# One transformer block on one core: the router's logits by expert in the later halves, batch 1's projections moved among the maxima, the last output projection half a pass later

## The reference, cut to what matters

```
def expert_choice_ffn(x, gate_w, w_gate, w_up, w_down):     # B=4, S=1024, D=128, 8 experts, I=512
    affinity = softmax(x @ gate_w.T)                        # over the 8 experts
    gating, idx = top_k(affinity.transpose(0, 2, 1), 256)   # each expert takes 256 tokens of each batch
    x_in = x[idx]
    h = silu(x_in @ w_gate.T) * (x_in @ w_up.T)
    return zeros.at[idx].add(gating * (h @ w_down.T))

x = x + 0.5 * expert_choice_ffn(layernorm(x))
x = x + attention(layernorm(x))   # 16 heads of 8, 3D rotary turn of q and k, softmax over 1024 keys, then Wo
x = x + 0.5 * expert_choice_ffn(layernorm(x))
```

## Time and profile before

| | |
|---|---|
| median of 3 executions | 1208.99 us (1207.38 to 1209.43) |
| the profiled execution | 1207.35 us, of it 1205.3 us span |
| start, first halves' front | 0 to 66 us |
| first expert layer | 66 to 298.5 us |
| window, 44 pieces of the maxima | 298.5 to 362 us |
| attention's main loop | 362 to 962 us |
| second expert layer, last scatter ends | 971 to 1198.5 us |
| busy: TensorE, VectorE, ScalarE, GpSimd | 1088.2, 918.8, 769.6, 600.1 us |

### The profile page before, as it was taken

One profiled execution on the slowest core, in us unless ns is written; L12 is line 12 of the kernel. 1 busy time (PEld: TensorE's weight loads), 2 busy tenths in 40 slices (PEclk: granted clock), 3 DMA queues, 4 the chain that ended last, 5 costly groups with the idle time before them and its releaser, 6 DMA issues.

```text
span 1205.3 us, 23761 instructions
## 1 busy us (share of the span) xinstructions
PE 1088.2 (90%) x8900; PEld 478.3 (40%) x8900; DVE 918.8 (76%) x1510; ACT 769.6 (64%) x1461; POOL 600.1 (50%) x619
## 2 busy tenths in 40 slices
PE   6199999898599999999999999999998889999993
PEld 6167666565132222222222222222222256666762
DVE  5745855465979999999999999999997554854441
ACT  3054322432368999999989999899999836222220
POOL 4046888775378511100003447455430187677886
PEclk6579999999598999999999999999999988999997
DMA  9025456458514220212111222112310125345553
GB/s 274 32 60 115 91 112 136 88 118 198 135 37 123 61 64 19 58 46 58 40 29 40 52 52 62 25 40 58 81 45 8 31 79 130 83 92 101 114 101 30
DMA packets 93065, 93.95 MB, mean 78 GB/s; under 512 B 14684, under 2 KB 70108, under 8 KB 92920
## 3 DMA queue, kind: packets, MB, share of 16 engines
q1 hardware_dynamic: 70424, 75.66, 22.6%
q0 software_dynamic: 22528, 16.79, 10.3%
HBM read 64.22 MB, written 30.13 MB: 78 GB/s over the span
## 4 chain that ended last, share of the span: by engine, by line
DVE 43%; PE 35%; issue 11%; POOL 5%; ACT 4%; DMA 1%; SPq 0%; DVEq 0%; POOLq 0%; another core or an unknown queue 0%; ACTq 0%
DVE mx L1877 38%; PE pA L1329 7%; PE pS L1317 7%; POOL out_dram L655 3%; ACT Pt L1154 3%; PE pO L1318 3%; PE pS L1318 3%; PE pO L1469 3%; DVE ge L1564 2%; PE pS L1490 2%; PE pA L1297 2%; PE pS L1235 2%; POOL xg L632 1%; PE pA L1405 1%; PE pA L1235 1%
## 5 line engine op out<-in xcount | busy, mean ns | idle before, releaser
L1877 DVE TENSOR_REDUCE mx<-pA 128x2 f32<-128x1024 f32 x512 | 585.2, 1217 | 13.8 <-PE pA L1405 13.0
L1154 ACT ACTIVATE Pt<-pS 128x512 f32<-128x512 f32 x1024 | 556.3, 596 | 30.9 <-PE pS L1490 25.0
L1469 PE MATMUL pO<-Pt,Vst 128*16 128x256 f32 x4096 | 321.5, 386 | 12.5 <-ACT U L1145 12.5
L1049 ACT ACTIVATE Pt<-pS 128x512 f32<-128x512 f32 x128 | 76.4, 597 | 199.9 <-PE pS L1317 176.6
L632 POOL DMA_INDIRECT xg<-zd,idx x128 | 128.4, 1003 | 149.4 <-DVE idx L1684 76.3
L1405 PE MATMUL pA<-Kst,Qst 48*128 48x512 bf16 x704 | 140.9, 397 | 20.1 <-DVE mx L1877 18.9
L1469 PEld LDWEIGHTS pO<-Pt,Vst 128*16 128x16 f32 x4096 | 68.0, 94 | 204.3 <-issue 107.2
L1317 PE MATMUL pS<-Pt,wg 128*128 128x512 f32 x256 | 139.7, 628 | 4.5 <-DVE Pt L1711 2.1
L1490 PE MATMUL pS<-Qst,Kst 51*128 51x512 bf16 x704 | 138.6, 390 | 5.1 <-issue 1.0
L722 POOL TENSOR_TENSOR mparts<-mx,onesm 128x32 bf16<-128x32 f32 x16 | 4.0, 252 | 267.1 <-DVE mx L1882 210.9
L1329 PEld LDWEIGHTS pA<-wd,Pt 128*128 128x128 f32 x960 | 113.5, 192 | 16.8 <-issue 16.8
(11 more groups left out here) (229 smaller groups left out, 1214.7 us busy)
## 6 DMA issues: line engine op xcount, KB each, us to landing
wg<-w_gate_dram SPq DMA_DIRECT2D x32, 256.0 KB
wu<-w_up_dram SPq DMA_DIRECT2D x32, 256.0 KB
wd<-w_down_dram SPq DMA_DIRECT2D x32, 256.0 KB
qk<-parts SPq DMA_DIRECT2D x64, 96.0 KB
Kst<-qk SPq DMA_DIRECT2D x132, 32.0 KB
zd<-Z SPq DMA_DIRECT2D x8, 512.0 KB
vp<-pair SPq DMA_DIRECT2D x4, 1024.0 KB, 4.6
Vst<-vp SPq DMA_DIRECT2D x16, 256.0 KB
```

Source lines behind the costliest of these rows:

```text
L1049: S.activation(sg[:, u % 2, :], pG[u % 2], ACT.Silu).then_inc(s_silu, 1)
L1154: S.activation(Pt[:, s % 4, j, r * 512:(r + 1) * 512], pS[:, bank_of(k, 4 * s + 2 * j + r), :], ACT.Exp, scale=SCALE).then_inc(s_exp, 1)
L1469: last = M.matmul(pO[32 * h:32 * h + 16, cols], Vst[k][:, s % 8, h, :], Pt[:, s % 4, h // 2, (h % 2) * 512 + 256 * a:(h % 2) * 512 + 256 * ...
L1877: V.reduce_max(mx2[:, k, 2 * j:2 * j + 2, c, half], pA[ring[q, a] % 2][:, :, :], AX.X).then_inc(s_Ar, 1)
```

## The change

Five edits.

1. `veps` is gone: the root is taken of the variance itself, with 1e-5 as the activation's bias, from a tile `eps` that GpSimd fills at the start.
2. For the second half of each layer (hh = 1 and 3) the logits come with the experts on the rows: `gate_t`, padded to 32 columns, is the weight, and 512 tokens at a time are streamed, four such matmuls in four column tiles of the array. ScalarE moves the bank to SBUF, and four transposes at n = 4 turn it. The new use `("g", hh)` stands at (1, 4) and (18, 4).
3. The projections of u = 2 and 3 leave passes 14 and 15 (`("s", 15)` to `("s", 24)`) and stand in the window, behind pieces 0 to 13. VectorE's eight multiplications and two sums for them go to ScalarE (8 moves) and GpSimd (4 products, 2 sums).
4. `("p", 3, 0)` goes from (16, 2) to (16, 4), `("p", 3, 1)` from (16, 4) to (17, 1). VectorE's and ScalarE's work around them follows. Of `("f", 3, n)`, n = 2 to 5 go later, and the search takes five gaps of passes 20 and 21 in place of four.
5. On SyncE `store_values(0)` goes behind `load_weights(15)`, `store_values(1)` behind the loads of x, `load_weights(18)` ahead of `write_out(3)`.

```diff
@@ tables
+    place[1, 4] = ("g", 1)
-    for m in range(5, 25):
+    for m in range(5, 15):
         place[divmod(55 + m, 5)] = ("s", m)
-    place[16, 2], place[16, 4] = ("p", 3, 0), ("p", 3, 1)
-    for n, at in enumerate([(17, 3), (17, 4), (18, 0), (18, 1), (18, 2), (18, 4)] + [(19, k) for k in range(5)] +
-                           [(it, k) for it in (20, 21) for k in range(4)] + [(22, 0), (22, 1)]):
+    place[16, 4], place[17, 1] = ("p", 3, 0), ("p", 3, 1)
+    for n, at in enumerate([(17, 3), (17, 4), (18, 2), (18, 3), (19, 0), (19, 1)] + [(19, k) for k in range(2, 5)] +
+                           [(it, k) for it in (20, 21) for k in range(5)] + [(22, 0), (22, 1)]):
         place[at] = ("f", 3, n)
+    place[18, 4] = ("g", 3)
...
-    for u, at in ((4, 22), (5, 28), (6, 32), (7, 37)):
-        for i in range(4):
-            window[divmod(at + i, 32)] = ("PR", u, i)
+    for u, ats in ((2, (0, 2, 4, 6)), (3, (8, 10, 12, 13)), (4, range(22, 26)), (5, range(28, 32)), (6, range(32, 36)), (7, range(37, 41))):
+        for i, at in enumerate(ats):
+            window[divmod(at, 32)] = ("PR", u, i)
@@ SyncE
-            store_values(0)
             store_parts(0)
             load_weights(15)
+            store_values(0)
             store_parts(1)
             load(0)
             load(1)
-            store_values(1)
...
+            store_values(1)
             store_parts(2)
...
+            load_weights(18)
             write_out(3)
-            load_weights(18)
@@ GpSimd
             scatter(RUN - 1)
+            product(2, 0)
+            product(2, 1)
+            add_products(2)
+            product(3, 0)
             rest(2)
+            product(3, 1)
+            add_products(3)
+            lowest(2)
             rest(3)
-            lowest(2)
             lowest(3)
@@ ScalarE
-                S.activation(sd[:, tiles(i)], veps[:, tiles(i)], ACT.Sqrt).then_inc(s_sd, 1)
+                S.activation(sd[:, tiles(i)], mv[:, tiles(i), 1], ACT.Sqrt, bias=eps[:, 0:1]).then_inc(s_sd, 1)
...
+                if key and key[0] == "g":
+                    act.wait_ge(*written(key))
+                    S.activation(by_expert, sidebank, ACT.Copy).then_inc(s_room, 1)
...
+            for u in (2, 3):
+                for i in range(4):
+                    projected(u, i)
+                value_rows(u)
+            high(2)
             deviation(6)
+            middle(2)
             deviation(7)
@@ TensorE
+            def logits_by_expert(hh):
+                bank, sem = open_bank(("g", hh))
+                pe.wait_ge(*was_read(("f", hh, 3)))
+                for g in range(4):
+                    last = M.matmul(bank[32 * g:32 * g + 32, :], gate_t[:, :], ZT[:, g * 512:(g + 1) * 512], start=True, stop=True,
+                                    tile_position=(0, 32 * g))
+                last.then_inc(sem, 1)
...
-                pe.wait_ge(*was_read(("s", 24) if j < RUN else ("f", 3, NF - 1)))
+                pe.wait_ge(*was_read(("s", 14) if j < RUN else ("f", 3, NF - 1)))
...
-            pe.wait_ge(s_vs, 4)
+            pe.wait_ge(s_vs, 6)
@@ VectorE
                 for n in ts:
                     last = V.bn_aggr(mv[:, n, :], stats[:, n % CH, :])
-                link(last)
-                V.tensor_scalar(veps[:, tiles(i)], mv[:, tiles(i), 1], EPS, None, ALU.add).then_inc(s_ve, 1)
+                last.then_inc(s_ve, 1)
```

More of the change, by code:

```diff
@@ L113, in program @@
         stats = sb("stats", [P, CH, 6], F32)
-        veps = sb("veps", [P, T], F32)
+        eps = sb("eps", [P, 1], F32)
         sd = sb("sd", [P, T], F32)
@@ L217, in program @@
         num, den = scr[:, 0:2, :], scr[:, 2:4, :]
-        pairs = {4: (scr[:, 0, :], scr[:, 2, :]), 5: (scr[:, 1, :], scr[:, 3, :]), 6: (room[:, 0, :], room[:, 1, :]),
-                 7: (U[1][:, :], U[2][:, :])}
+        pairs = {u: (scr[:, u % 2, :], scr[:, 2 + u % 2, :]) for u in range(2, 6)}
+        pairs |= {6: (room[:, 0, :], room[:, 1, :]),
+                  7: (U[1][:, :], U[2][:, :])}
         dens = sb("dens", [P, P], F32)
@@ L1107, in _ @@
             normalise(6)
+            high(3)
             turned_half(0)
             turned_half(1)
+            middle(3)
             normalise(7)
@@ L1202, in front @@
                     if hh:
[L1203 to L1207, removed]
+                        pe.wait_ge(*was_read(("g", hh)))
+                        for k in range(4):
+                            last = M.transpose(bank[:, k * P:(k + 1) * P], by_expert[:, k * P:(k + 1) * P], ident[:, :])
+                    else:
+                        for k in range(CH, HT):
+                            if k % 4 == 0:
+                                pe.wait_ge(*was_read(("f", 0, k // 4)))
+                            last = M.matmul(bank[:, k * E:(k + 1) * E], ZT[:, k * P:(k + 1) * P], gate_t[:, 0:E], start=True, stop=True)
                 elif n < 7:
@@ L1277, in use @@
                     front(key[1], key[2])
+                elif key[0] == "g":
+                    logits_by_expert(key[1])
                 elif key[0] == "s":
@@ L1387, in _ @@
                     pe.wait_ge(*was_read(("f", 0, k // 4)))
-                M.matmul(bank_of_use(("f", 0, 4))[:, k * E:(k + 1) * E], ZT[:, k * P:(k + 1) * P], gate_t[:, :], start=True, stop=True)
+                M.matmul(bank_of_use(("f", 0, 4))[:, k * E:(k + 1) * E], ZT[:, k * P:(k + 1) * P], gate_t[:, 0:E], start=True, stop=True)
             for n in range(2, 8):
@@ L1429, in window_use @@
                     if i == 0:
-                        pe.wait_ge(s_winr, win["T", 2 * (b - 2) + 1] + 1)
-                    last = project(op, (wq, wr)[i // 2], 2 * (b - 2) + i % 2, bank)
+                        pe.wait_ge(*(was_read(("s", 4)) if b == 1 else (s_winr, win["T", 2 * (b - 2) + 1] + 1)))
+                    last = project(op, (wq, wr)[i // 2], 2 * (b % 2) + i % 2, bank)
                 else:
@@ L1437, in window_use @@
                     u = key[1]
[L1438 to L1439 removed]
+                    if u > 2:
+                        pe.wait_ge(s_vs, u - 2)
                     project_values(u, pO[:, :]).then_inc(s_v, 1)
@@ L1546, in moments @@
                 ts = range(i % B * CH, (i % B + 1) * CH)
+                if i:
+                    dve.wait_ge(s_ve, nth(i) - 1)
                 for n in ts:
@@ L1584, in front @@
                 if n == 4:
-                    logits = bank[:, 0:HT * E].rearrange("p (t e) -> p t e", e=E)
-                    link(V.reduce_max(lmax[:, :], logits, AX.X))
-                    V.tensor_tensor(lsub[:, :, :], logits, lmax[:, :].unsqueeze(2).to_broadcast([P, HT, E]),
-                                    ALU.subtract).then_inc(signal_read(key), 1)
+                    if hh:
+                        logits = bank.rearrange("p (j g r) -> p g j r", j=4, g=4)[:, :, :, 0:E]
+                    else:
+                        logits = bank[:, 0:HT * E].rearrange("p (g j e) -> p g j e", j=4, g=4)
+                    largest_of = lmax[:, :].rearrange("p (g j) -> p g j", j=4)
+                    link(V.reduce_max(largest_of, logits, AX.X))
+                    V.tensor_tensor(lsub[:, :, :].rearrange("p (g j) e -> p g j e", j=4), logits,
+                                    largest_of.unsqueeze(3).to_broadcast([P, 4, 4, E]), ALU.subtract).then_inc(signal_read(key), 1)
                     affinities(hh)
```

49 lines of the change are left out of this document (25 added, 24 removed).

## The result

The changed kernel takes 1198.72 us (median of 4, 1197.10 to 1199.40) against 1208.96 us: the ratio is 0.9916, with a 95% interval from 0.9898 to 0.9933. That is 10.2 us less, where 12.1 were forecast, and the time lies in the range. The profiled execution has a span of 1195.3 us, with a mean granted clock of 0.953.

What follows compares the result with a forecast made beforehand. VectorE was taken to bound the attention and TensorE the expert layers, GpSimd close behind. The terms -0.6 - 2.0 - 7.0 - 2.5 = -12.1 gave 1195.25 us for the profiled execution, 1196.9 for the median; range 1190 to 1204.

Steps and rivals of the forecast that it cites:

- The root without its addition: At the kernel's start, VectorE's addition of 0.69 us ahead of ScalarE's root goes: -0.6 us.
- later uses stand beside other work: Dropping the addition at roots after the kernel's start was taken to gain 0.
- Logits by expert: First layer: the logits' 3.49 us on TensorE become 1.10 plus 0.43 for transposes: -2.0 us, from 0 to -2.5.
- Passes 14 and 15: Batch 1's projections leave these passes, so the maxima start at 290.0 instead of 298.54: -8.5 us.
- the wait for `load(0)`: Before the maxima: the load would land some 4 us after TensorE is ready, between 288.5 and 292.5.
- TensorE's 10.1: What TensorE alone would gain from passes 14 and 15, with the maxima starting at 288.5: 10.1 us.
- SyncE's reordered stores: They have free stretches around them: 0, if the values' stores land before the maxima's values are used.
- The window: Attention's start, with the moved projections: some run at half clock, GpSimd's work fits: +1.5 us, from 0 to +4.
- the 7.0 of the sum: Net of moving batch 1's projections into the window: -7.0 us, from -10 to -2.
- Second layer: Later last projection and new logits: -0.8 + 1.9 - 5.3 + 1.7 = -2.5 us, from -6 to 0.
- the attention's start gives back: Rival, 1201 to 1205 us: late `load(0)`, GpSimd's 2.3 us margin used up, half clock costing +4; chance 0.15.
- the half clock through the whole window: Rival: TensorE stays at half clock in the whole window, +28.8 us there, 1224 in all; chance 0.07.

Runs made afterwards that it cites:

- a_veps: The changed kernel without edit 1, so VectorE adds the constant again before each root: 1197.78 us, ratio 0.9925 to the kernel before.
- b_proj: The kernel before with edit 3 alone, plus only the move of `store_values(1)` that it needs: 1202.45 us, ratio 0.9966.
- a_sum_early: The changed kernel with VectorE's last sum of batch 0's parts one gap sooner and its store ahead of the last down weights' load: 1196.95 us, ratio 0.9913.
- a_again: The changed kernel timed and profiled once more, with no edit: 1198.16 us, ratio 0.9923 to the kernel before.
- best_a: a_sum_early with the window's two shift operations reading the reciprocal from PSUM, written there by one more reciprocal each: 1192.77 us, ratio 0.9884.
- best_b: The same as best_a, with edit 4 taken back: 1191.33 us, ratio 0.9872 to the kernel before.

## Why the prediction was right, and where it was not

**The root without its addition, -0.6.** In this pair of profiles the front is 0.55 shorter. But in kernels that are alike there it is from 0.7 us longer to 1.0 shorter than before's, and a_veps is no slower. The size was right for the operation and can't be told in the time. What I priced at nothing, "later uses stand beside other work", is wrong: in the window the addition waits for GpSimd (1.78 us in b_proj, 1.98 in a_veps, for 0.17).

**Logits by expert, -2.0.** 2.4 to 2.5 us between the compactions of passes 1 and 2 in all ten kernels that have it. The group takes 1.07 us, next to the 1.10 estimated from the earlier trace rows; the rest is the idle before the old logits. So the tiling rule of the Trainium skill ("TensorEngine Tiling (Array Packing)", Key Properties) costs no more here than the 0.09 us by which the group begins later (91.49) than the next matmul would, 0.86 behind 90.54.

**Passes 14 and 15, -8.5, and the wait for `load(0)`.** The mechanism was right: TensorE's 10.1 is reached in a_sum_early, and in the changed kernel a wait of 3.85 us for the load takes part of it, leaving 7.2 to 7.7. What I mis-sized is how much sooner the load comes. The compaction of pass 13 is 5.2 us sooner than before. VectorE's sum of the parts gains 2.4 us on that (I had up to 3), and SyncE's store starts with its end:

```profile
264.39 1.13 DVE L1736 TENSOR_SCALAR Pt<-pA,gain 128x128 f32<-128x128 f32 x4 [2.34 <-PE pA L1366]
265.43 1.22 DVE L1787 TENSOR_TENSOR parts<-scr,parts 128x1024 bf16<-128x1024 f32 x1
```

But the eight issues of this store take 5.54 us (5.36 in a_again), where they took 3.89, so that `load(0)` begins at 275.13 for 280.91, only 0.5 us more than the 5.2 sooner. In a_sum_early they take 3.90 again. Why they took longer is open. The sum itself still stood behind a scaling that had waited 2.34 us for the down projection. And SyncE's reordered stores, for which I had 0, probably carry a part, as b_proj's pass 15 shows.

**The window, +1.5 from the clock.** Size near (+2.2 and +2.3; +1.1 to +3.6 over the five kernels with this window), cause in good part wrong. I counted GpSimd's time and asked only whether it would finish (34.6 us after the start; my own terms add up to 34.8). It finished later, with its first product 39.8 us after the start (36.9 before), and nothing on TensorE waited for it. I did not ask what it would do to VectorE while it runs: the shifts cost 1.8 us more, in each of the five. The trace of the kernel before had shown it, in pass 17, where GpSimd writes the second half of its `Z` from 996.76 to 997.80:

```profile
996.84 0.98 DVE L1560 SCALAR_TENSOR_TENSOR shift<-mv,rstd 128x8 f32<-128x8 f32 x1
```

The clock's part at the start is the two slow projections ahead of 291.23, by their excess over 1.13 some 1.2 us at most. What differs between the five goes with the clock from 31 to 41 us after the first piece, where TensorE is full: 0.50 in the longest window (67.4), 0.63 in this one, 0.70 in the shortest (64.9). Together with the load this makes the net of edit 3 5.0 and 5.4 us in the two profiles and 4 to 6 in the timed kernels, for the 7.0 of the sum.

**Second layer, -2.5.** This step failed: the stretch is no shorter. From the first score matmul to the last scatter the stretch took 834.6 and 831.7 us in the two kernels in which it is unchanged (before, b_proj), and 832.5 to 834.8, mean 833.7, in seven with both edits. The single terms came: the wait for GpSimd's `Z` came (4.46 us), with a clock of 0.50 behind it, the logits and the half clock behind them went, and the search's waits grew by 1.6 us (4.15 for 2.53 from pass 19's compaction on), where I had 1.7. (From the compaction of pass 19 to that of pass 22 all nine profiles with edit 4 are 2.6 to 3.1 us longer than before's, the four others without it are from 0.4 shorter to 0.1 longer; what is not waits is in part steps of the front that edit 4 moves into this stretch.) What I had not is 1.24 us for the gathered tokens and 1.4 us by which GpSimd reaches `Z` later than TensorE's shift would have it (the starts on TensorE are 10.8 us sooner at 949.94, and 9.4 at 988.14). Its tree of sums before that took longer in this profile: 3.13 and 4.71 us for the groups that took 2.28 and 3.61. The single sums that stretched ran beside VectorE's `tensor_tensor` operations with two SBUF inputs: one of 0.26 us took 0.76 beside `room<-slots,place_in`. That these are the operations which edit 4 moved is not shown: in b_proj, without edit 4, the groups took 2.99 and 4.44 us. Which of edits 2 and 4 gives what in this layer stays open to about 1.5 us: kernels alike in it differ by more.

**Why the total was right** is then partly luck: 2.5 forecast for the second layer and 2 too many for edit 3 were missing, and 0.9 us in pass 0, 2.0 in pass 11 and 0.5 more at the logits came in unforecast in this profile, less 0.7 in the first layer's search. By the timed kernels edit 2 is worth 4.7 to 5.5 us in all, where the profiles show 2.5 and an uncertain rest.

Of the rivals, that the attention's start gives back was true in part, for the load and not for GpSimd's margin; the half clock through the whole window did not come, since the clock was 1.00 from 292 to 302 already.

## What to carry to other kernels

When work is moved onto an engine that rests, ask not only whether it is done in time but what it holds while it runs: six operations that met no deadline problem stretched two tiny ones, on the engine that bounds the stretch, sixfold. An operand in PSUM took them out of its way for 0.4 us. Look in the old profile for the same operation beside the same engine: it stood there with 0.98 us. When the bound engine is relieved, follow the next one back to the instruction that releases it, and to what is queued in front of that: here a load waited for a store, the store for a sum, and the sum stood behind a scaling that waited for TensorE. And profile one kernel twice before a difference of 2 us between two profiles is explained.

## What the runs showed of the hardware

A small VectorE operation with two SBUF inputs that starts while a GpSimd `tensor_tensor` runs ends with it (310.87 beside 310.84, 313.28 beside 313.26, 310.92 beside 310.90), and doesn't wait if one of its inputs lies in PSUM (0.16 us, twice in best_a and twice in best_b). A larger one waits too: in the kernel before the 128x512 product of the context, for which TensorE waited 3.21 us, took 2.25 us beside a GpSimd operation, and 0.69 us without one. `reduce_max` from PSUM, the batch statistics and the reciprocal kept their times. The Trainium skill says this in "SBUF — State Buffer", Who interferes with whom (a VectorE instruction with two SBUF inputs contends with a GpSimd instruction that reads SBUF, and the second to issue blocks), and the trace agrees in every case; I had read it ahead of the prediction as a rule about `reduce_max`, which never contends, and left it out. The `tensor_scalar` with one SBUF input was held up too (0.37, 1.78 and 1.98 us for 0.17).

Two profiles of one program differed by 4.8 us in one unchanged stretch, up to the compaction of pass 11: an estimated 1.7 us by the granted clock (0.92 and 1.00), the rest by TensorE's waits for gathered tokens, for `Z` and for VectorE (6.5 and 3.6 us).
